# Identity products ahead of transposed scores, two scatters in flight, and a group of heads weighed at once, in a two-layer adaLN kernel

## The chip, the cores and the metric

The kernel runs on one core of a Trainium2 chip. The metric is the time of one execution in microseconds, the lower the better. TensorE multiplies, VectorE and ScalarE work elementwise, GpSimd fills tables and issues the indirect transfers, SyncE issues the plain ones.

## The reference

2,048 tokens of 128 channels go through two layers, each with an attention-like part and a mixture of experts, each part on a layer norm with a modulation (scale, shift, gate).

- Layer 0, attention: the tokens are taken as sequences, and only the first 256 to 309 rows take part. 16 heads of 8 channels. Three passes: a query is projected and normalised for each head, scores against all keys in a window are taken through a softmax, the values are weighed, and the result is added to the query. The window of the next pass is 256, 281 or 309 rows, by how much the result moved.
- Layer 0, experts: softmax router, two of eight experts for each token, 128 to 512 to 128 channels with GELU.
- Layer 1, in place of attention: a linear recurrence with 32 complex modes. Experts: one of eight, ReLU.

```python
scores = einsum('bhqd,bhkd->bhqk', sq, sk) * inv_sqrt_e      # in the window
probs = softmax(scores, axis=-1)
out = einsum('bhqk,bhkd->bhqd', probs, vp)
...                                                            # three passes
y = einsum('nec,ne->nc', out_of_experts, combine)              # two of eight experts
```

## The kernel before

All engines run their own written-out program; semaphores order them. 16 tiles of 128 tokens. The first three tiles (`NA = 3`, "near") take part in attention; the other 13 ("far") do not, and are made ready while attention runs.

**The three passes** (`attend(it)` on each engine). In a pass `nj` is the number of query or key tiles (2, 3, 3) and `nw` the window (256, 281, 309). VectorE makes the normalised queries (`head_norm`, `split`) into a stack, which TensorE turns (`turn`), and ScalarE or VectorE copies. Then come the *scores*: for each head TensorE forms `nj` products into PSUM banks `3b .. 3b+2`, `b = h % 2` (`scores`, L1035), and VectorE reduces them to the row maxima (`maxima`, L1775), which are put into the stack and turned in again. Then the *transposed scores* (`scores_t`, L1055): the same products with keys on the partitions, of which ScalarE takes the exponential (L777) as soon as one of the two bank groups is written. TensorE weighs the values with them (`weigh_one`, L1060): each head writes 9 rows at partition `32 q` of a bank, so that four heads share a bank. `weigh_four(g, jk)` does one key tile of the four heads of group `g`. ScalarE copies the bank (`take`, L784), and TensorE turns it out (`turn_out`, L1082) with a map. VectorE then divides and goes on to the next pass.

`fill(bank, count)` (L1015) is a product of the identity with a repeated identity, 512 columns, into a bank that is about to be overwritten; its result is not used. Before the change it stands ahead of the scores of heads 2 to 15 of passes 1 and 2, and in runs at the start of passes.

For the first three groups, `weigh_four` is mixed with the transposed scores of later heads. The last group is done head by head: after head 2 of the group the groups 0 and 1 are turned out, then head 3 is weighed.

**The far rows.** During pass 0 VectorE adds the bias to all of x and normalises the far rows; TensorE and ScalarE run the router between pass 0 and 1; in pass 1 VectorE chooses experts, counts (TensorE, `count("far")`) and computes the row that each token has in the sorted buffer (`place`). Then GpSimd writes the far rows there with an indirect transfer of 128 rows for each tile and choice, 2 x 13 = 26 (`send_row`, L585). Each waits until the one before has landed. After the first 13 a column of the rows is rewritten (`set_places`). SyncE waits for all 26 (`wait_scattered`) and then loads sorted tiles of 128 rows.

**The experts** (`experts(l)`): turn a tile (L1231), four products up (L1247), bias on VectorE (L1920), activation on ScalarE, four products down (L1258). They start after the attention output was added to the near rows and these are normalised, all on VectorE ahead of its first expert bias. The near rows are routed during the first nine tiles. Layer 1 then follows with a scatter of its own, 16 transfers with no wait between them.

## Time and profile before

| | us |
|---|---|
| three timed runs | 446.42, 459.40, 461.73 |
| their median | 459.4 |
| the profiled execution | 444.71 |
| its span, first to last instruction | 442.7 |
| TensorE, VectorE busy in it | 309.9, 304.5 |
| mean granted TensorE clock in it | 0.822 of 2.4 GHz |

The profile is of one execution. Busy times overlap between engines and do not add up to the span.

### The profile page before, as it was taken

The page shows a single profiled execution, that of the slowest core. Times are in us where ns is not written, and L with a number is a line of the kernel's source. Part 1 is how long each engine was busy: PE and PEld are TensorE (multiplying, and loading weights), DVE is VectorE, ACT ScalarE, POOL GpSimd, SP SyncE. Part 2 cuts the span into 40 slices and gives each one's busy share as a digit, 9 for nine tenths or more (in the row PEclk, how much of TensorE's full clock was granted, in tenths as well). Part 3 has the DMA queues.
Part 4 walks back from the last instruction along what each step waited for, and adds up shares of the span by engine and source line. Part 5 has one row for each costly group of instructions (what it writes and reads, how often), then busy time and mean ns, then how long its engine had stood idle before and what let it go on. Part 6 is the DMA issues. An engine that isn't in the chain of part 4 may idle for free.

```text
span 442.7 us, 7609 instructions
## 1 busy us (share of the span) xinstructions
PE 309.9 (70%) x2168; PEld 222.3 (50%) x2169; DVE 304.5 (69%) x859; ACT 172.0 (39%) x331; POOL 172.4 (39%) x281
## 2 busy tenths in 40 slices
PE   1896888788997889778788999216807200699960
PEld 1672216332353322478788999203807100689960
DVE  7598985995869994268755666566979760277850
ACT  1134553217601268053354555846024600345520
POOL 9572880740133344303575455300000087044560
PEclk9997559697999988969899999758775555699995
DMA  2599800000000000031224220694000022323310
GB/s 79 94 365 371 243 3 1 0 1 1 8 24 24 32 18 26 29 59 44 60 62 79 70 68 28 180 305 135 0 1 1 0 75 106 89 67 82 96 51 0
DMA packets 37805, 32.93 MB, mean 74 GB/s; under 512 B 10765, under 2 KB 28770, under 8 KB 37776
## 3 DMA queue, kind: packets, MB, share of 16 engines
q1 hardware_dynamic: 33792, 25.10, 20.3%
q0 software_dynamic: 3936, 7.49, 5.4%
q8 instruction: 13, 0.21, 0.2%
q14 instruction: 16, 0.13, 0.1%
q10 hardware_dynamic: 48, 0.00, 0.0%
HBM read 19.50 MB, written 13.98 MB: 76 GB/s over the span
## 4 chain that ended last, share of the span: by engine, by line
PE 36%; DVE 24%; DMA 18%; issue 7%; ACT 6%; POOL 4%; SPq 2%; DVEq 1%; POOLq 0%
DMA rows<-token_rows,posu 15%; PE ps L1247 12%; PE ps L1258 10%; POOL rows L585 4%; DVE mx L1775 3%; PE ps L1060 3%; PE ps L1055 2%; PE ps L1035 2%; DVE stats L1383 2%; PE ps L1231 2%; DMA xs<-rows 2%; SPq L293 1%; DVE wide L2017 1%; PE ps L1215 1%; DVE hb L1920 1%
## 5 line engine op out<-in xcount | busy, mean ns | idle before, releaser
L585 POOL DMA_INDIRECT rows<-token_rows,posu x48 | 50.5, 1053 | 142.3 <-DVE token_rows L1698 71.4
L1258 PE MATMUL ps<-w_out,hg 128*128 x496 | 66.1, 278 | 0.0
L1920 DVE TENSOR_TENSOR hb<-ps,b_in 128x512 f32<-128x512 f32 x62 | 42.7, 688 | 31.7 <-PE ps L1247 31.3
L1258 PEld LDWEIGHTS ps<-w_out,hg 128*128 128x128 f32 x496 | 61.0, 194 | 0.2
L597 POOL DMA_INDIRECT back<-ys,places x39 | 38.5, 988 | 48.5 <-DVE ys L1931 43.4
L866 ACT ACTIVATE hg<-hb 128x512 f32<-128x512 f32 x62 | 39.1, 630 | 37.5 <-DVE hb L1920 32.9
L1775 DVE TENSOR_REDUCE mx<-ps 128x2 f32<-128x512 f32 (+2 forms) x48 | 44.1, 947 | 2.3 <-PE ps L1035 1.7
L1247 PE MATMUL ps<-xsT,w_now 128*128 128x128 f32 x256 | 39.2, 302 | 5.9 <-DVE hb L1920 3.7
L1231 PE MATMUL ps<-ident,xs 128*128 128x128 f32 x62 | 18.1, 296 | 35.1 <-DMA xs<-rows 35.1
L1247 PEld LDWEIGHTS ps<-xsT,w_now 128*128 128x128 f32 x256 | 35.2, 213 | 7.5 <-issue 5.1
L765 ACT COPY qs<-ps 128x768 bf16<-128x768 bf16 (+1 forms) x21 | 15.3, 729 | 59.7 <-PE ps L1004 59.7
L597 POOL DMA_INDIRECT out<-ys,rest x23 | 22.6, 984 | 33.2 <-DVE ys L1939 29.3
L1247 PE MATMUL ps<-xsT,qs 128*128 128x128 f32 x240 | 32.1, 277 | 1.0 <-DVE hb L1920 1.0
L1015 PE MATMUL ps<-identb 128*128 128x512 bf16 x98 | 27.5, 392 | 5.6 <-DVE mx L1775 5.2
L1055 PE MATMUL ps<-qs,feat 64*128 64x281 bf16 (+2 forms) x128 | 26.8, 348 | 5.3 <-ACT wide L777 4.1
L1247 PEld LDWEIGHTS ps<-xsT,qs 128*128 128x128 f32 x240 | 29.5, 194 | 1.1 <-issue 1.1
L857 ACT ACTIVATE xsT<-ps,modcol 128x128 f32<-128x128 f32 x39 | 17.7, 454 | 30.3 <-PE ps L1231 30.2
L1931 DVE TENSOR_TENSOR ys<-ps,b_out 128x128 f32<-128x128 f32 x62 | 17.9, 289 | 16.1 <-PE ps L1258 15.0
L777 ACT ACTIVATE wide<-ps 128x512 f32<-128x512 f32 (+2 forms) x36 | 27.5, 819 | 3.6 <-PE ps L1055 3.6
L1231 PEld LDWEIGHTS ps<-ident,xs 128*128 128x128 f32 x62 | 9.4, 152 | 36.2 <-issue 34.2
L1060 PE MATMUL ps<-wide,vpx 128*9 128x281 f32 (+2 forms) x192 | 27.1, 526 | 0.1
L1035 PE MATMUL ps<-feat,qs 64*128 64x281 bf16 (+2 forms) x128 | 24.7, 319 | 3.3 <-DVE mx L1775 1.9
(390 smaller groups left out, 570.4 us busy)
## 6 DMA issues: line engine op xcount, KB each, us to landing
rows<-blank SPq DMA_DIRECT2D x20, 260.0 KB, 7.3
xs<-rows SPq DMA_DIRECT2D x62, 64.0 KB
w_in<-in_L_ffn_w_fc SPq DMA_DIRECT2D x1, 2048.0 KB, 15.1
w_in<-in_L_ffn_W SPq DMA_DIRECT2D x1, 2048.0 KB, 10.5
rest<-rows SPq DMA_DIRECT2D x23, 65.0 KB
token_rows<-in_L_attn_x SPq DMA_DIRECT2D x1, 832.0 KB, 8.1
wmod<-in_L_wmod SPq DMA_DIRECT2D x2, 384.0 KB, 4.3
rows<-token_rows,posu POOLq DMA_INDIRECT x48, 2.4
```

Of the source, the lines that this page charges most:

```text
L585: pool.indirect_dma_start(ROWS[l], bass.IndirectOffsetOnAxis(ap=posu[:, k, j:j + 1], axis=0), token_rows[:, j, 0:WIDTH[l]], None).then_inc ...
L597: pool.indirect_dma_start(where, bass.IndirectOffsetOnAxis(ap=target[r] if l else places[:, t, :].bitcast(U32)[:, 0:1], axis=0), ys[:, r, ...
L777: act.activation(probs[h % NPROBS][:, 0:nj, 0:nw], ps[:, 3 * b:3 * b + nj, 0:nw], ACT.Exp).then_inc(sem("probs_ready"), 1)
L866: act.activation(hg[:, c % RING, :], hb[:, c % 2, :], fn).then_inc(sem("hg_ready"), 1)
L1035: mm = pe.matmul(ps[:, 3 * b + j, 0:nw], half(qs, h)[:, j * P:(j + 1) * P], half(ks, h)[:, 0:nw], start=True, stop=True)
L1055: mm = pe.matmul(ps[:, 3 * b + j, 0:nw], half(ks, h)[:, j * P:(j + 1) * P], half(qs, h)[:, 0:nw], start=True, stop=True)
L1060: return pe.matmul(ps[OROW * q:OROW * q + HD + 1, 6 + g % 2, 0:nw], vpx[:, jk, h, :], probs[h % NPROBS][:, jk, 0:nw], start=(jk == 0), sto ...
L1231: pe.transpose(ps[:, 4 + c % 2, 0:P], xs[:, c % RING, :], ident[:]).then_inc(sem("xs_used"), 1)
L1247: mm = pe.matmul(ps[:, b, n * P:(n + 1) * P], w_ring[c % RING][:, n * P:(n + 1) * P], xsT[:, c % 2, :], start=True, stop=True)
L1258: mm = pe.matmul(ps[:, 6 + c % 2, 0:D], hg[:, c % RING, n * P:(n + 1) * P], w_out[:, bass.ds(e * NB + n, 1), :], start=(n == 0), stop=(n = ...
L1775: v.tensor_reduce(mx[:, 0:nj, h:h + 1], ps[:, 3 * b:3 * b + nj, 0:nw], AX.X, ALU.max).then_inc(sem("max_free"), 1)
L1920: v.tensor_tensor(hb[:, c % 2, :].rearrange("p (b t) -> p b t", b=NB), ps[:, c % RING if h_bank(l, t) is None else h_bank(l, t), :].rearra ...
```

## The change

1. `scores` puts an identity product ahead of heads 2 to 15 in pass 0 too (14 more). `scores_t` puts one ahead of heads 0 to 7, in all three passes (24 more).
2. The far transfers alternate between two semaphores. Each waits only for the one before the last, so two are in flight. Between the two halves both semaphores are waited for, as before; SyncE waits for both.
3. The last group of heads is weighed as the others are, with three (or two) calls of `weigh_four`, after groups 0 and 1 are turned out. `turn_out(0)` now waits for the exponential of head 14, the last even one, and `weigh_four(3, 0)` for that of head 15.

```diff
@@ wait_scattered (SyncE)
-                    sp.wait_ge(sem("scattered_" + g), 16 * (hi - lo) * experts)
+                    n = (hi - lo) * experts
+                    if g == "far":
+                        sp.wait_ge(sem("scattered_odd"), 16 * (n // 2))
+                        n -= n // 2
+                    sp.wait_ge(sem("scattered_" + g), 16 * n)
@@ send_row (GpSimd)
-                                        token_rows[:, j, 0:WIDTH[l]], None).then_inc(sem("scattered_" + g), 16)
+                                        token_rows[:, j, 0:WIDTH[l]], None).then_inc(sem("scattered_odd" if odd else "scattered_" + g), 16)
@@ the far scatter (GpSimd)
-                    pool.wait_ge(sem("scattered_far"), 16 * sent)
+                    pool.wait_ge(sem("scattered_far"), 16 * (sent - sent // 2))
+                    pool.wait_ge(sem("scattered_odd"), 16 * (sent // 2))
                     set_places(NA, NT, N)
                     pool.wait_ge(sem("places_set"), 3)
                 for j in range(NA, NT):
-                    if j > NA:
-                        pool.wait_ge(sem("scattered_far"), 16 * sent)
-                    send_row("far", 0, k, j)
+                    if sent > 1:
+                        pool.wait_ge(sem(("scattered_far", "scattered_odd")[sent % 2]), 16 * (sent // 2))
+                    send_row("far", 0, k, j, odd=bool(sent % 2))
                     sent += 1
@@ scores (TensorE)
-                        if it and h >= 2:
+                        if h >= 2:
                             fill(3 * b, 1)
@@ scores_t (TensorE)
+                        if h < 8:
+                            fill(3 * b, 1)
@@ the end of attend (TensorE)
-                pe.wait_ge(sem("o_taken"), G0 + 2)
-                for q in range(4):
-                    if q == 3:
-
-                        turn_out(0)
-                        turn_out(1)
-                    pe.wait_ge(sem("probs_ready"), H0 + 13 + q)
-                    for jk in range(nj):
-                        mm = weigh_one(3, q, jk)
-                mm.then_inc(sem("weighed"), 1)
+                pe.wait_ge(sem("probs_ready"), H0 + HEADS - 1)
+                turn_out(0)
+                turn_out(1)
+                for jk in range(nj):
+                    weigh_four(3, jk)
                 turn_out(2)
                 turn_out(3).then_inc(sem("o_turned"), 1)
```

## Rows read from the trace of the kernel before

**Rows 1.** The chain that ended last, in time: start us, us, what

```profile
118.44 3.14 DMA rows<-token_rows,posu
...
186.52 2.29 DMA rows<-token_rows,posu
188.82 1.80 DMA xs<-rows
```

**Rows 2.** Timeline of VectorE: start us, us, instruction, [idle before, releaser]

```profile
188.15 0.56 DVE L1880 TENSOR_TENSOR token_rows<-token_rows,ps 128x384 f32<-128x384 f32 x1 [1.74 <-PE ps L1208]
...
191.58 0.86 DVE L1402 TENSOR_SCALAR token_rows<-token_rows,mv,rstd 128x128 f32<-128x128 f32 x3
...
193.97 0.69 DVE L1920 TENSOR_TENSOR hb<-ps,b_in 128x512 f32<-128x512 f32 x1 [0.61 <-PE ps L1247]
```

**Rows 3.** Windows: us, busy time of PE, PEld, DVE, ACT, POOL, granted clock, DMA

```profile
42.00:66.00 24.00, 20.57 (x117) 5.20 (x116) 22.00 (x75) 13.92 (x25) 19.05 (x53) 0.50 0.49 150
80.00:84.00 4.00, 3.77 (x21) 1.79 (x19) 3.61 (x11) 0.80 (x1) 3.82 (x5) 0.50 0.00 0
84.00:100.00 16.00, 13.22 (x84) 5.46 (x80) 15.67 (x20) 3.19 (x4) 9.79 (x8) 0.99 0.00 1
104.00:112.00 8.00, 7.33 (x48) 1.91 (x52) 2.22 (x12) 5.13 (x8) 0.00 (x0) 0.57 0.01 2
162.00:169.00 7.00, 7.00 (x47) 1.46 (x46) 6.79 (x9) 4.38 (x6) 3.62 (x3) 0.55 0.07 21
```

**Rows 4.** The chain that ended last, in the scatter of layer 1

```profile
363.69 0.96 POOL rows L585
364.95 0.96 POOL rows L585
```

**Rows 5.** Timelines of TensorE and ScalarE, end of pass 2

```profile
175.05 2.00 PE L1060 MATMUL ps<-wide,vpx 128*9 128x309 f32 x16
...
178.29 1.55 PE L1082 MATMUL ps<-omap,wmod 128*128 128x68 f32 x12
179.77 1.73 PE L1060 MATMUL ps<-hg,vpx 128*9 128x309 f32 x6
181.43 1.55 PE L1082 MATMUL ps<-omap,wmod 128*128 128x68 f32 x12
...
175.21 0.94 ACT L777 ACTIVATE hg<-ps 128x927 f32<-128x927 f32 x1 [0.18 <-PE ps L1055]
```

**Rows 6.** Timeline of TensorE, pass 1

```profile
81.53 1.91 PE L1015 MATMUL ps<-identb 128*128 128x512 bf16 x4
...
108.03 1.13 PE L1060 MATMUL ps<-wide,vpx 128*9 128x281 f32 x8
109.09 0.88 PE L1055 MATMUL ps<-qs,feat 64*128 64x281 bf16 x3
...
117.04 0.66 PE L1060 MATMUL ps<-wide,vpx 128*9 128x281 f32 x8
117.63 0.53 PE L1055 MATMUL ps<-qs,feat 64*128 64x281 bf16 x3
118.09 0.66 PE L1060 MATMUL ps<-wide,vpx 128*9 128x281 f32 x8
...
124.06 1.55 PE L1082 MATMUL ps<-omap,wmod 128*128 128x68 f32 x12
```

**Rows 7.** Timelines of VectorE and TensorE, pass 0

```profile
42.61 2.07 DVE L1775 TENSOR_REDUCE mx<-ps 128x2 f32<-128x512 f32 x3
...
45.75 2.08 DVE L1775 TENSOR_REDUCE mx<-ps 128x2 f32<-128x512 f32 x3
...
70.90 0.19 DVE L1715 TENSOR_SCALAR den<-ps 128x32 f32<-128x32 f32 x1 [5.42 <-PE ps L1082]
...
62.64 0.60 PE L1055 MATMUL ps<-qs,feat 64*128 64x256 bf16 x2 [0.74 <-ACT wide L777]
...
64.14 0.60 PE L1055 MATMUL ps<-qs,feat 64*128 64x256 bf16 x2
```

More of the change, by code:

```diff
@@ L581, in ready_to_send, with send_row @@
                 pool.wait_ge(sem(f"cleared{l}"), 16 * clears(l))
-            def send_row(g, l, k, j):
+            def send_row(g, l, k, j, odd=False):
                 pool.indirect_dma_start(ROWS[l], bass.IndirectOffsetOnAxis(ap=posu[:, k, j:j + 1], axis=0),
-                                        token_rows[:, j, 0:WIDTH[l]], None).then_inc(sem("scattered_" + g), 16)
+                                        token_rows[:, j, 0:WIDTH[l]], None).then_inc(sem("scattered_odd" if odd else "scattered_" + g), 16)
             def send_tile(l, t):
```

## The prediction

> **What bounds the kernel now.** I read the chain of work that ended last first. From 118 to 189 us it is one thing, the scatter of the far token rows: 26 transfers from 118.44 to 186.52 us, a mean spacing of 68.08 / 25 = 2.72 us, each step being a landing of about 2.29 us and then the next issue, and behind the last one the first load of sorted rows at 188.82 us [rows 1]. The reader is to see that nothing of TensorE or VectorE stands in the chain there. Second, the timelines of VectorE and TensorE at the same place, to see what is late next: the third attention pass ends with the add of 188.15 us and a layer norm until 191.58 + 0.86 = 192.44 us, and the first expert bias comes at 193.97 after only 0.61 us of waiting for TensorE [rows 2]. So scatter and attention tie: making the scatter alone shorter frees about 3 us, making the attention alone shorter frees nothing once the scatter is issued. What is worth something is both together. Third, the windows with the granted clock: TensorE stands at half speed (1.2 GHz) from 42 to 66 us, at 80 to 84, and for most of 104 to 112 and 162 to 169 us [rows 3].
>
> **Two far transfers in flight.** Removed: 24 of the 26 waits for the transfer before; added: a wait for the last but one. A transfer lands 2.29 us after its issue and the wait and issue around it take 0.26 more. With two in flight the spacing is the larger of 2.55 / 2 = 1.28 us and what GpSimd itself needs. The second layer's scatter shows the latter without any wait between issues: 363.69 to 364.95 us, 1.26 us, with rows twice as wide [rows 4]. I take 1.3 us, bounds 1.26 (GpSimd) and 2.55 (no overlap), nearer the lower one because the only row without waits shows it. The drain between the two halves stays, so 26 x 1.3 + 3 = 37 us instead of 70.4. Behind these waits GpSimd has the sends of the first expert results, due only once the experts run, and SyncE the row loads, which want the scatter done anyway, so nothing else is delayed. The saving, 33 us, is not the gain: the attention pass covers all but the last 3 us. It only takes the scatter out of the way of what follows.
>
> **The last four heads weighed together.** In pass 2 the last weighing of the third group starts at 175.05 and takes about 0.7 us; from there the serial form (three heads, the turning out of two groups, the fourth head) lasts until 181.43: 5.7 us. The new order is the turning out of groups 0 and 1, 179.77 - 178.29 = 1.48 us, and three four-head weighings of 0.66 us (0.73 at 309 columns) [rows 5, 6], 3.4 to 3.7 us. Saved: 2.0 to 2.3, I take 2.2. Pass 1 by the same rows: from 118.09 + 0.66 to 124.06 is 5.3 us, the new order 1.48 + 3 x 0.6 = 3.3; saved 2.0. The added wait, all four exponentials before any of the weighing, costs nothing as long as the turning out covers it: the last exponential ends at 175.21 + 0.94 = 176.15 us [rows 5], the turning out would run to about 177.2; if that cover were gone, it would cost at most the 0.9 us of one exponential. Behind it on TensorE only the end of the pass is queued. Pass 0 has two key tiles instead of three; its small saving (0 to 1 us) falls under the cap below. What is late next is ScalarE's copy of the last group, which keeps its place, and then VectorE, which idles in front of it in every pass.
>
> **Identity products, passes 1 and 2.** Eight more of 512 columns in each pass, ahead of heads 0 to 7 of the transposed scores. At half speed four take 1.91 us, 0.48 each [rows 6]; at full speed I halve that, 0.24. What they may buy is the half-speed stretch that follows. A pair of weighing and scores costs 1.13 + 0.88 us at half speed and 0.66 + 0.53 at full [rows 6], 0.47 and 0.35 less. The stretch of pass 1 holds three weighings and four scores: 3 x 0.47 + 4 x 0.35 = 2.8 us, minus the four products that now stand in it, 4 x 0.24: 1.9 us. Pass 2 has a stretch of about the same length; I allow 0.2 us for products that ScalarE has to wait for ahead of it: 1.7 us. Bounds for each pass: +3.4 (the whole stretch at double speed, products hidden) and -3.8 (8 x 0.48, no change of clock and no cover). Why near the upper end: from 84 to 100 us the products of the first scores hold 0.99 with TensorE 83% busy, and this cadence is what the transposed scores now get; in the 4 us before, dense products at half speed were followed by full speed [rows 3].
>
> **Identity products, pass 0.** 14 in front of the scores and 8 in front of the transposed scores. The pass enters the scores at half speed. There VectorE's reductions set the pace, four heads in 45.75 - 42.61 = 3.14 us [rows 7]; with a product per head TensorE needs about 0.48 for the two score products of 256 columns (together one identity product long), 0.48 for the identity product and 0.1 for its share of the turning, 1.05 us per head, so it becomes the bound and each head loses 0.25 us until the clock rises. I put the rise 4 to 7 us later, as at 80 to 84 us [rows 3]: 1.0 to 1.7 us lost, and about 0.07 per head won afterwards because the waits of VectorE go: net -0.9 us. The transposed part now takes 1.50 us per head from head 6 on (62.64 to 64.14) [rows 7], all of it TensorE at half speed; at 2.4 GHz it takes half, 0.75, or up to 0.85 where ScalarE sets the pace (my allowance), over ten heads 6.5 to 7.5 us less. Not all counts. VectorE does the layer norm of the far rows meanwhile and is idle only 5.42 us before it takes the result at 70.90 [rows 7]; that idle time is a cap on everything saved in the second half of pass 0, the new weighing included. So pass 0 gives 5.4 - 0.9 = 4.5 us; bounds -5 (no rise) and +5.4.
>
> Of this part the Trainium skill says in "TensorE: Matmul & The Clock Gate", Terms, that the penalty of the throttle is about the time throttled times what is missing of the clock. By it pass 0 alone would give 24 x 0.5 = 12 us; the 5.42 us of VectorE speak against that in this kernel.
>
> **Entry to the experts.** With the far rows long in memory the first turned tile no longer waits for a load. TensorE would have the first tiles' products ready when the layer norm ends, and VectorE's 0.61 us of waiting goes [rows 2], and some of that before the second and third bias. The sum of the removed waits is at least 0.6 and at most 2.7 (TensorE's turn is set by a load that came 188.82 + 1.80 = 190.62, against an attention end near 188) [rows 1, 2]; I take 1.5. From there on the order of work is unchanged and I carry the gain through to the end.
>
> **The sum.** 4.5 (pass 0) + 1.9 + 2.0 (pass 1) + 1.7 + 2.2 (pass 2) + 1.5 (entry) = 13.8 us. The check on the scatter: it can start 4.5 + 1.9 = 6.4 us earlier, at 112.0, and ends near 149; the attention ends near 188.0 - 12.3 = 175.7. The scatter would bind again only above (175.7 - 112.0) / 26 = 2.45 us per transfer. The profiled execution took 444.7 us with a span of 442.7; it goes to 430.9, span 428.9. The three timed runs are 446.4, 459.4 and 461.7, so the profile belongs with the lowest, and the median is 3% above it; the traces do not say why. From the lowest run the sum gives 432.6, which is my forecast, 433; from the median it would give 445.6, which the range must hold. A gain below about 2%, 9 us, could not be told from none.
>
> **Pass 0 stays at half speed.** For it: that pass ran at 0.50 for 24 us though TensorE was 86% busy [rows 3]. Against: with the products it becomes the bound, and is idle no more. It would lose 14 x 0.25 + 8 x 0.2, about 5 us, instead of winning 4.5: 13.8 - 9.5 = 4.3 saved, 440. Chance 0.15.
> **Slower: the products never lift the clock and nothing hides them.** Place: before the exponentials, where ScalarE waits for each score. Price: 5 us in pass 0 and 3.8 in each of the others, with the half-speed stretches kept, against 4.2 from the weighing and 1.5 at the entry: 12.6 - 5.7 = 7 us slower, 452. It decides from the point at which fewer than about one in two of the 38 products is covered. Chance 0.05.
> **The transfers do not overlap.** The change then does not do what it says: spacing 2.55, the scatter ends 6.4 us earlier and no more, and so does the start of the experts: 438. Against: the scatter of the second layer [rows 4]. Chance 0.08.
> **The clock counts in full.** All half-speed time is halved: 12 + 3.4 + 3.1 us, and 5.7 for weighing and entry: 24 us, 420. This is what the rule cited above amounts to. It would need VectorE's work in pass 0 off the path [rows 7]. Chance 0.05.
> The forecast has 0.60; the rest, 0.07, is anything else.
>
> **How the numbers follow.** Low end 425: the upper bounds of passes 1 and 2 and of the entry. High end 449: the forecast counted from the median of the runs with some of the fills uncovered, the half-speed rival included. Faster by over 2%: the forecast, the full clock and the part of the others that lies beyond, 0.72; within 2%: 0.23; slower 0.05.
>
> **What would show it.** Right: far scatter of about 37 us with spacings of 1.3; granted clock 1.0 from about 46 us on in pass 0 and through the transposed scores of passes 1 and 2; TensorE's last turning out within 4 us of the last group's third weighing; VectorE idle under 1 us before it takes the result of pass 0; the first turned tile right behind the attention output. Wrong: 0.50 anywhere in the transposed scores, or a longer mean of the exponential's waits without a higher clock, or a later wait in the experts that takes back what the entry gained.

## The result, and the profile after

The changed kernel takes 473.12 us (median of four executions, 467.11 to 477.58) against 455.27 us of the kernel before (446.42 to 461.73): a ratio of 1.050 with a 95% interval of 1.027 to 1.072. Every ratio here leaves out executions that lie well above the fastest of their kernel, so it is not the quotient of the two medians, which is 1.039. The kernel is slower, outside my range of 425 to 449. The profiled execution took 477.58 us, the highest of its four, as that of before was the lowest of its own, so the two spans (475.9 and 442.7 us) lie 33 us apart where the medians lie 18: what the two profiles differ by is more than the change costs on the median.

The page of the changed kernel: span, busy time, and the granted clock in tenths in 40 slices.

```profile
span 475.9 us, 7691 instructions
PE 346.6 (73%) x2206; PEld 229.5 (48%) x2207; DVE 304.1 (64%) x859; ACT 173.3 (36%) x331; POOL 170.3 (36%) x281
PEclk9796556755589955597997999975775555599995
```

TensorE is busy 37 us longer with 38 more small products, which alone would be 9 to 21 us (38 at 0.24 to 0.54): the rest is the same work at a lower clock, 0.745 on the mean against 0.822. The windows say where. Columns as in [rows 3]; the first answers to its 42:66, the third and fourth are the scores (all but their first 2.3 us) and transposed scores of pass 1, the last two those of pass 2.

```profile
42.00:66.00 24.00, 24.00 (x93) 6.19 (x91) 18.04 (x57) 9.95 (x16) 18.07 (x53) 0.50 0.51 158
66.00:80.00 14.00, 12.57 (x82) 3.90 (x77) 4.87 (x20) 6.08 (x14) 0.91 (x2) 0.51 0.00 1
97.00:117.00 20.00, 20.00 (x77) 7.09 (x76) 14.20 (x17) 2.42 (x4) 7.26 (x6) 0.50 0.00 0
117.00:132.00 15.00, 15.00 (x68) 4.19 (x69) 4.45 (x20) 8.85 (x11) 0.00 (x0) 0.50 0.01 1
162.00:185.00 23.00, 21.91 (x86) 7.54 (x83) 17.86 (x19) 3.41 (x6) 10.64 (x11) 0.57 0.21 44
185.00:203.00 18.00, 18.00 (x83) 4.66 (x86) 13.25 (x23) 11.12 (x13) 0.00 (x0) 0.51 0.00 1
```

Passes 1 and 2 enter their scores (94.67 and 162.00) at full speed and lose it there, near 97 and 165 us. It comes back in the later part of each pass only, near 134.4 and 202.7 us. Narrow windows around the two falls:

```profile
94.00:96.00 2.00, 0.80 (x9) 0.43 (x7) 1.93 (x4) 0.80 (x1) 1.82 (x3) 1.00 0.00 0
96.00:98.00 2.00, 1.91 (x9) 0.62 (x9) 1.68 (x2) 0.00 (x0) 2.00 (x2) 0.71 0.00 0
164.00:166.00 2.00, 1.86 (x12) 0.92 (x11) 2.00 (x3) 0.15 (x1) 1.36 (x3) 0.78 0.11 33
```

The first window of the table above is the surprise: TensorE is busy for 24.00 of 24 us, where it was 20.57, and the clock stays at 1.2 GHz throughout; VectorE, the bound before with 22.00, is down to 18.04. The timeline of TensorE there:

```profile
42.75 0.61 PE L1040 MATMUL ps<-feat,qs 64*128 64x256 bf16 x2
43.29 0.61 PE L1020 MATMUL ps<-identb 128*128 128x512 bf16 x1
43.83 0.61 PE L1040 MATMUL ps<-feat,qs 64*128 64x256 bf16 x2
44.37 0.61 PE L1020 MATMUL ps<-identb 128*128 128x512 bf16 x1
```

Starts are 0.54 us apart, so a head takes 1.08 us where VectorE could take one in 3.14 / 4 = 0.79 [rows 7]. VectorE's wait for the result of the pass, 5.42 us in [rows 7], is now 10.07:

```profile
81.18 0.19 DVE L1717 TENSOR_SCALAR den<-ps 128x32 f32<-128x32 f32 x1 [10.07 <-PE ps L1089]
```

The scatter does what the change says. Its issues on GpSimd, which answer to [rows 1], are mostly 1.28 us apart (2.56 before; 2.72 on the mean, the drain between the halves included), and it is issued in 36.7 us, from 138.9 to 175.5. The first load of sorted rows starts at 177.9, long before the last add of the attention at 218.6:

```profile
147.06 0.97 POOL L589 DMA_INDIRECT rows<-token_rows,posu  x1 [0.30 <-DMA rows<-token_rows,posu]
148.34 0.97 POOL L589 DMA_INDIRECT rows<-token_rows,posu  x1 [0.31 <-issue]
149.63 0.98 POOL L589 DMA_INDIRECT rows<-token_rows,posu  x1 [0.32 <-issue]
...
175.52 0.97 POOL L589 DMA_INDIRECT rows<-token_rows,posu  x1 [0.31 <-issue]
```

So does the weighing. TensorE at the ends of pass 1 and pass 2, against [rows 6] and [rows 5]: from the last weighing of the third group (139.14 and 208.00) to the last turning out (142.76 and 211.80) it is 3.0 and 3.1 us where it was 5.3 and 5.7. But in pass 1 TensorE stops in the middle of that turning out:

```profile
139.14 0.66 PE L1067 MATMUL ps<-wide,vpx 128*9 128x281 f32 x8
139.73 1.55 PE L1089 MATMUL ps<-omap,wmod 128*128 128x68 f32 x12
...
142.76 0.89 PE L1089 MATMUL ps<-omap,wmod 128*128 128x68 f32 x6
145.79 0.89 PE L1089 MATMUL ps<-omap,wmod 128*128 128x68 f32 x6 [2.15 <-issue]
...
208.00 0.71 PE L1067 MATMUL ps<-wide,vpx 128*9 128x309 f32 x8
208.63 1.55 PE L1089 MATMUL ps<-omap,wmod 128*128 128x68 f32 x12
...
211.80 1.55 PE L1089 MATMUL ps<-omap,wmod 128*128 128x68 f32 x12
```

It waits for ScalarE's copy of the last group. That copy, ready to go when the weighing ended near 142.8, runs only at 145.34, 2.5 us late, and the releaser named is none of this core's engines:

```profile
145.34 0.39 ACT L789 COPY wmod<-ps 128x281 f32<-128x281 f32 x1 [4.88 <-remote]
```

At the entry to the experts VectorE no longer waits for TensorE, as forecast (0.61 us in [rows 2], nothing here):

```profile
218.59 0.56 DVE L1882 TENSOR_TENSOR token_rows<-token_rows,ps 128x384 f32<-128x384 f32 x1 [1.81 <-PE ps L1210]
...
223.72 0.68 DVE L1922 TENSOR_TENSOR hb<-ps,b_in 128x512 f32<-128x512 f32 x1
```

I followed one set of milestones through every profile: the first and last row maximum of a pass, the start of VectorE's `den` that takes the pass's result, the far counts (after the transposed scores of pass 1), the first expert bias. The table gives the time from one to the next, in us, read from the timelines (two ways between passes, 13.5 and 14.6 us before, are left out); "1/2" marks stages at half speed, or at half speed but for their first 2 to 4 us. Each column is one execution: "after" the longest of its four, "no scatter" the shortest of its six. Forecasts are the terms of the prediction.

| stage | before | after | forecast | before again | no scatter edit |
|---|---|---|---|---|---|
| pass 0, scores | 12.1 | 17.9 | | 12.1 | 17.5 |
| pass 0, from last maximum to result | 19.9 | 24.4 | (pass 0: -4.5) | 20.5 | 25.1 |
| pass 1, scores | 16.9 | 22.6 (1/2) | | 16.9 | 16.9 |
| pass 1, transposed scores | 10.1 | 14.6 (1/2) | -1.9 | 10.1 | 8.6 |
| pass 1, weighing to result | 14.3 | 15.8 | -2.0 | 14.6 | 11.8 |
| pass 2, scores | 17.4 | 23.3 (1/2) | | 17.4 | 17.4 |
| pass 2, from last maximum to result | 25.3 | 28.1 | -3.9 | 25.3 | 21.4 |
| result of pass 2 to first bias | 10.9 | 10.3 | -1.5 | 13.1 | 20.2 |
| end of span | 442.7 | 475.9 | | 450.6 | 456.8 |

### The profile page after: what moved, and what is told of

Same layout as the page of the kernel before. It is cut to its first block, busy times and chain, and to the rows that moved or that the text cites. A ratio compares the mean times of both kernels' runs of the same rounds, so it can differ in the third digit from the quotient of the medians.

```text
span 475.9 us, 7691 instructions
## 1 busy us (share of the span) xinstructions
PE 346.6 (73%) x2206; PEld 229.5 (48%) x2207; DVE 304.1 (64%) x859; ACT 173.3 (36%) x331; POOL 170.3 (36%) x281
## 4 chain that ended last, share of the span: by engine, by line
PE 50%; DVE 26%; issue 9%; POOL 5%; ACT 2%; DMA 2%; DVEq 2%; SPq 1%; another core or an unknown queue 1%; POOLq 0%
PE ps L1249 9%; PE ps L1260 7%; PE ps L1020 7%; PE ps L1040 6%; PE ps L1062 6%; PE ps L1067 5%; POOL rows L589 3%; DVE hb L1922 2%; PE ps L1009 2%; PE ps L1089 2%; DVE stats L1385 2%; SPq L293 1%; POOL out L601 1%; DVE wide L2019 1%; PE ps L1217 1%
## 5 line engine op out<-in xcount | busy, mean ns | idle before, releaser
L589 POOL DMA_INDIRECT rows<-token_rows,posu x48 | 49.4, 1030 | 122.4 <-DVE token_rows L1700 71.6
L1922 DVE TENSOR_TENSOR hb<-ps,b_in 128x512 f32<-128x512 f32 x62 | 42.5, 686 | 33.4 <-PE ps L1249 25.1
L1020 PE MATMUL ps<-identb 128*128 128x512 bf16 x136 | 56.3, 494 | 2.7 <-DVE mx L1777 2.5
L1777 DVE TENSOR_REDUCE mx<-ps 128x2 f32<-128x512 f32 (+2 forms) x48 | 45.2, 950 | 18.2 <-PE ps L1040 16.8
L1040 PE MATMUL ps<-feat,qs 64*128 64x281 bf16 (+2 forms) x128 | 34.5, 403 | 1.0 <-DVE qs L1763 1.0
L601 POOL DMA_INDIRECT out<-ys,rest x23 | 22.6, 983 | 33.3 <-DVE ys L1941 22.6
L1062 PE MATMUL ps<-qs,feat 64*128 64x281 bf16 (+2 forms) x128 | 32.1, 395 | 1.4 <-ACT wide L782 0.7
L782 ACT ACTIVATE wide<-ps 128x512 f32<-128x512 f32 (+2 forms) x36 | 28.6, 807 | 12.1 <-PE ps L1062 12.1
L1020 PEld LDWEIGHTS ps<-identb 128*128 128x128 bf16 x136 | 14.5, 108 | 35.4 <-DVE mx L1777 11.7
L1933 DVE TENSOR_TENSOR ys<-ps,b_out 128x128 f32<-128x128 f32 x62 | 17.8, 287 | 18.4 <-PE ps L1260 14.2
L862 ACT ACTIVATE xsT<-ps,modcol 128x128 f32<-128x128 f32 x39 | 17.5, 452 | 32.4 <-PE ps L1233 26.4
## 6 DMA issues: line engine op xcount, KB each, us to landing
w_in<-in_L_ffn_W SPq DMA_DIRECT2D x1, 2048.0 KB, 10.3
```

The lines of the kernel that those rows point to most:

```text
L589: pool.indirect_dma_start(ROWS[l], bass.IndirectOffsetOnAxis(ap=posu[:, k, j:j + 1], axis=0), token_rows[:, j, 0:WIDTH[l]], None).then_inc ...
L601: pool.indirect_dma_start(where, bass.IndirectOffsetOnAxis(ap=target[r] if l else places[:, t, :].bitcast(U32)[:, 0:1], axis=0), ys[:, r, ...
L782: act.activation(probs[h % NPROBS][:, 0:nj, 0:nw], ps[:, 3 * b:3 * b + nj, 0:nw], ACT.Exp).then_inc(sem("probs_ready"), 1)
L1020: pe.matmul(ps[:, bank, :], identb[:], identb[:].unsqueeze(1).to_broadcast([P, 4, P]), start=True, stop=True)
L1040: mm = pe.matmul(ps[:, 3 * b + j, 0:nw], half(qs, h)[:, j * P:(j + 1) * P], half(ks, h)[:, 0:nw], start=True, stop=True)
L1062: mm = pe.matmul(ps[:, 3 * b + j, 0:nw], half(ks, h)[:, j * P:(j + 1) * P], half(qs, h)[:, 0:nw], start=True, stop=True)
```

## The experiments

Every run is told with its median, the number of executions, and the ratio to the kernel before on the same chip. The edits are pieces of the change on the kernel before unless the text says otherwise.

### The kernel before again

> The kernel before once more, for a second profile. If the first profile was a lucky one (theory H: full speed through the scores of passes 1 and 2 is chance), this one has at least one of the two at 0.50 and 22.7 us in place of 16.9 there, and takes 450 to 462 us. If not, it takes about 445 us with the same stretches of half speed.

453.14 us (n 11), ratio 0.997 [0.992, 1.002]. Its profile has a span of 450.6 us with a clock of 0.80. In the runs beside the parts the kernel before had 78 more executions between 446.7 and 466.8 us. The profile from which I forecast, 444.71 us, was below every one of them. Its 8 us are hardly in the passes (0.9 up to the result of pass 2) but from the entry to the experts on. So the starting point of the forecast was about 10 us too low, whatever the change did.

### One part alone: products in pass 0

```diff
-                        if it and h >= 2:
+                        if h >= 2:
                             fill(3 * b, 1)
```

> The kernel before with the 14 identity products ahead of the scores of pass 0 and nothing else. Theory A (at half speed a stream of identity products and score products does not raise the clock): pass 0 stays at 0.50 and each head of the scores takes 1.09 us instead of 0.79, about 4 to 5 us slower. Theory C (the half speed of pass 0 in the changed kernel was chance of that one profile): the clock rises within 7 us and the kernel gains up to 5 us.

456.64 us (n 4), ratio 1.008 [1.001, 1.016]. Scores of pass 0: 17.9 us, as in the changed kernel; the rest of the pass as before (20.0); pass 1 and 2 unchanged (16.9, 17.4). The clock is 0.50 from 42 to 66 us. The step "I put the rise 4 to 7 us later" fails already here, alone.

### One part alone: products ahead of the transposed scores

```diff
                             pe.wait_ge(sem("qs_act"), C0 + 4 + h // 4)
+                        if h < 8:
+                            fill(3 * b, 1)
```

> The kernel before with the 24 identity products ahead of the transposed scores and nothing else. Theory A: pass 0 is at half speed there, 8 products of 0.54 us are paid in full or nearly, 3 to 4 us slower in pass 0; in passes 1 and 2 they hold full speed if the clock is there and cost up to 4 us if it is not; in all 2 to 8 us slower. Theory D (they hold the clock in passes 1 and 2, as was forecast): pass 0 loses 3 us and passes 1 and 2 give 3 to 4 back, no difference.

458.77 us (n 4), ratio 1.012 [1.003, 1.020]. The profile is of the longest of the four. Pass 0, from last maximum to result: 24.5 us for 19.9, so eight products at half speed, 8 x 0.54 = 4.3, and nothing hides them. In pass 1 the clock fell inside the scores, at about 97 us (20.3 us for 16.9), and the transposed scores ran at half speed, 14.6 us for 10.1. Without these products they take 10.5 us at half speed (the profile of the two transfers in flight alone), so at that clock eight products cost 4.0 us there. In pass 2 at full speed they gained 1.4 us, near the forecast 1.7.

### The clock warm when pass 0 begins

Weighing and scatter as changed, products in the scores of pass 0, none ahead of the transposed scores, and a longer run of products at the start of the pass.

```diff
                     pe.wait_ge(sem("ks_act"), 4)
+                    fill(4, 5)
...
-                            fill(4, (12, 0, 44)[it])
+                            fill(4, (22, 0, 44)[it])
```

> The two other edits, the 14 products ahead of the scores of pass 0, and 15 more at the start of pass 0 that fill TensorE's idle time of 2.3 and 1.0 us there, so that the clock need not fall before the scores. Theory A (the products can hold full speed but not restore it): pass 0 at 1.00 through its scores at 0.72 us per head, and some way into the transposed scores; 3 to 8 us faster than the two edits alone in pass 0. Theory C' (products next to half-array score products can do neither): 0.50 from 40 us on, as in the changed kernel, 4 us slower than the two edits alone.

461.79 us (n 4), ratio 1.024 [1.007, 1.041], the denser scatter included. The windows, scores of pass 0 first, then the transposed part:

```profile
40.00:52.00 12.00, 10.99 (x64) 3.93 (x63) 10.81 (x19) 5.56 (x9) 5.69 (x24) 1.00 1.05 333
55.00:72.00 17.00, 15.57 (x102) 5.64 (x101) 11.13 (x49) 7.71 (x16) 11.19 (x24) 0.51 0.00 1
```

Entered at full speed, the mix held 1.00 here through the scores of pass 0; entered at half speed it held 0.50. And full speed buys nothing: the scores take 12.0 us for 12.1, since VectorE sets their pace (10.81 of 12 us busy). The clock fell again 3 us after them, at 55 us, when the weighing had started. That full speed is held is no rule: in pass 1 of this same profile the clock fell inside the scores, near 93 us.

### Four products a head in pass 0

```diff
-                        if it and h >= 2:
-                            fill(3 * b, 1)
+                        if h >= 2:
+                            fill(3 * b, 1 if it else 4)
```

> The kernel before with four identity products ahead of each of heads 2 to 15 of the scores of pass 0. Theory A1 (they can raise the clock if they are dense enough): 1.00 within some 7 us of their start, pass 0 then paced by 4 x 0.21 + 0.3 us per head, 1 to 5 us slower in all. Theory A2 (they cannot, whatever their number): 0.50 through all of them, 2.2 us per head and 20 us slower.

467.81 us (n 2), ratio 1.028 [1.017, 1.040]. TensorE at the point where the clock rises:

```profile
42.02 1.89 PE L1015 MATMUL ps<-identb 128*128 128x512 bf16 x4
43.84 0.61 PE L1035 MATMUL ps<-feat,qs 64*128 64x256 bf16 x2
44.38 0.61 PE L1004 MATMUL ps<-identb,stack 128*128 128x128 bf16 x4
44.78 1.34 PE L1015 MATMUL ps<-identb 128*128 128x512 bf16 x4
46.06 0.39 PE L1035 MATMUL ps<-feat,qs 64*128 64x256 bf16 x2
46.38 1.04 PE L1015 MATMUL ps<-identb 128*128 128x512 bf16 x4
```

Here it does rise, near 45 us; so the clock can be lifted in this stage, only not by one product a head. The price is a head every 1.29 us, 22.9 us for the scores, and at 66 us the clock is at half again.

### Products of ones in place of the identity

The changed kernel, with other data in the unused products only.

```diff
-                    pe.matmul(ps[:, bank, :], identb[:], identb[:].unsqueeze(1).to_broadcast([P, 4, P]), start=True, stop=True)
+                    pe.matmul(ps[:, bank, :], onesb[:], onesb[:].unsqueeze(1).to_broadcast([P, 4, P]), start=True, stop=True)
```

> The changed kernel with all its extra products taken as ones times ones instead of identity times identity; same sizes, same places. Theory F (what counts as activity is the data, and an identity is nearly all zeros): the clock rises in the scores of pass 0 and stays up, 10 to 25 us faster than the changed kernel. Theory G (the data do not matter): same time and same half-speed stretches as the changed kernel, about 473 us.

470.92 us (n 4), ratio 1.037 [1.014, 1.060]. The same window, the same picture, busy all the time at 0.50:

```profile
42.00:66.00 24.00, 24.00 (x91) 6.42 (x93) 17.76 (x55) 9.48 (x16) 17.60 (x52) 0.50 0.49 153
```

So the zeros of the identity are not what keeps the clock down in the scores of pass 0. Behind them this profile differs: the clock rises near 67 us, in the transposed scores (0.99 from 67 to 75), which none of the three profiles with identity products in both places shows before 78. Whether that is the data or chance, one profile does not tell.

### No products between heads

The kernel before without those it has in the scores of passes 1 and 2.

```diff
-                        if it and h >= 2:
-                            fill(3 * b, 1)
```

> The kernel before without the identity products that stand ahead of single heads in the scores of passes 1 and 2 (the runs of them at the start of passes stay). Theory A (bistable: with a product per head TensorE paces the scores at 1.36 us per head when at half speed and 1.05 when at full, without one VectorE paces them at 1.05 in either): scores of passes 1 and 2 at 1.05 us per head whatever the clock, spread of the runs smaller, median 0 to 6 us below the kernel before. Theory E (those products keep the clock up and are worth it): more half speed in the later part of each pass, 3 to 8 us slower.

456.91 us (n 4), ratio 1.012 [0.998, 1.027]. The scores of pass 1, at half speed for most of their time (0.58 on the mean), take 17.5 us: VectorE's pace, 0.6 us from full speed. Those of pass 2 take 18.4 for 17.4. With products they take 16.9 at full speed and 22.6 at half (table). So a product a head has two outcomes in these passes and is no insurance: in pass 1 it wins 0.6 us where the clock holds and costs 5.1 where it doesn't. The half-speed outcome is the one that lasts: once the clock had fallen inside these scores, no profile with products shows it back before they ended, and it fell there in the changed kernel and in several of its parts.

### One part alone: two transfers in flight

```diff
-                    if j > NA:
-                        pool.wait_ge(sem("scattered_far"), 16 * sent)
-                    send_row("far", 0, k, j)
+                    if sent > 1:
+                        pool.wait_ge(sem(("scattered_far", "scattered_odd")[sent % 2]), 16 * (sent // 2))
+                    send_row("far", 0, k, j, odd=bool(sent % 2))
```

> The kernel before with the two far transfers in flight and nothing else. Theory A (the identity products are what costs): the scatter shrinks from 70 to about 37 us, the attention pass covers all but the last 3 us of it, 0 to 3 us faster than before, and no new stall. Theory B (the denser scatter delays other transfers, the instruction fetch among them, as in the stall of 2 us while it ran in the changed kernel): 3 to 8 us slower, with idle time in the trace that no semaphore explains.

462.39 us (n 4), ratio 1.010 [0.996, 1.023]: no gain, though the scatter is issued in 37.3 us for 68.1. The profile is of the longest of the four. It names "issue" as the releaser of waits of, among others, 1.1 us on TensorE, 4.5 on VectorE and 4.7 on ScalarE in the stretch of the scatter, where the profiles of before and of the eight runs that keep its scatter have at most 0.2 us of that kind. Most of it is no delay. ScalarE's copy of the last group, in before and here:

```profile
124.16 0.39 ACT L784 COPY wmod<-ps 128x281 f32<-128x281 f32 x1 [4.74 <-PE ps L1060]
...
134.36 0.39 ACT L789 COPY wmod<-ps 128x281 f32<-128x281 f32 x1 [4.74 <-issue]
```

The same wait of 4.74 us, at the same place, ends at TensorE's product in one and has no name in the other. The same holds for the 1.1 us on TensorE (1.13 before, for VectorE), and VectorE's 4.5 us end 0.1 us after TensorE's turning out, as before. So a wait is to be compared with the same wait of before, not counted by its name. What is later in the way from pass 1 to pass 2 is 0.9 us in all, 15.5 us for 14.6.

Pass 2 then goes through its scores at half speed, 23.3 us for 17.4 (pass 1 did too, 22.7, ahead of the scatter):

```profile
155.00:175.00 20.00, 20.00 (x73) 6.66 (x71) 14.76 (x18) 3.17 (x5) 7.74 (x8) 0.50 0.22 45
```

### No wait at all between the transfers of a half

```diff
-                    if j > NA:
-                        pool.wait_ge(sem("scattered_far"), 16 * sent)
```

> The kernel before with no wait between the 13 transfers of a half (up to 13 in flight). Theory B (the fewer gaps the indirect transfers leave, the longer the instruction fetches of the other engines wait): more unexplained idle time on ScalarE, VectorE and TensorE from the start of the scatter on than with two in flight, and slower than before by 2 to 8 us. If GpSimd's own 1.27 us per transfer is what spaces them, the same as with two in flight. If theory B is wrong: no such idle time.

468.59 us (n 5), ratio 1.036 [1.026, 1.046], with one semaphore and no other edit. Up to the scatter (118.5 us) every milestone is that of before. Then VectorE's reductions of pass 2 stop, with no instruction of the profile to wait for:

```profile
147.41 1.13 DVE L1773 TENSOR_REDUCE mx<-ps 128x3 f32<-128x927 f32 x1 [0.30 <-PE ps L1033]
153.78 1.12 DVE L1773 TENSOR_REDUCE mx<-ps 128x3 f32<-128x927 f32 x1 [5.24 <-issue]
154.82 0.19 DVE L1767 CAST stack<-mx 128x12 bf16<-128x12 f32 x1
155.89 2.15 DVE L1773 TENSOR_REDUCE mx<-ps 128x3 f32<-128x927 f32 x2 [0.89 <-remote]
```

The scores of pass 2 take 28.7 us for 17.4, and the way into them 17.9 for 14.6. VectorE could start at 149.5, when the products were written, so it is 4.3 us late, and TensorE stands behind it:

```profile
154.96 0.61 PE L1013 MATMUL ps<-identb 128*128 128x512 bf16 x1 [5.48 <-DVE mx L1773]
```

The clock was 1.00 until this stop, falls near 152.5 us in it, and stays at 0.50 to the end of the scores. One wait was taken away, on GpSimd alone, so the denser transfers stop engines that have no part in them; this run alone does not tell their spacing from their number in flight.

### Two in flight, but spaced out

A memset of 0.54 us on GpSimd ahead of each transfer, into a buffer that is not in use yet.

```diff
+                    if j > NA:
+                        then(pool.memset(xs[:], 0.0))
                     send_row("far", 0, k, j, odd=bool(sent % 2))
```

> The kernel before with two far transfers in flight, but GpSimd clears an unused tile of 512 columns (about 0.7 us with its wait) between two issues, spacing some 2 us instead of 1.28. Theory B1 (the spacing is what counts): no unexplained waits on ScalarE and VectorE in pass 2, the scatter ends some 12 us earlier, pass 2 at full clock, the start of the experts 2 to 3 us earlier: 0 to 3 us faster than before. Theory B2 (two in flight is what counts): waits as with the unpaced scatter, 3 to 10 us slower.

454.33 us (n 11), ratio 1.009 [1.002, 1.015]. The spacing is 1.79 us (rows of it below, under the best version), the scatter is still issued in 49 us, and the scores of pass 2 keep their pace, 17.4 us at 1.00. The way from pass 1 to pass 2 is 15.9 us for 14.6. That is the price of the memset: VectorE's own instructions are slower while GpSimd writes. Four of them that compute `feat` take 2.51 us here for 1.88 in the repeated profile of before, and under the weighing as well three copies into the stack take 1.34 for 0.60. In this profile the spacing matters more than that two are in flight; the next paced kernels show how far that carries. It wins nothing alone, since the attention is next.

### The weighing alone

```diff
-                pe.wait_ge(sem("o_taken"), G0 + 2)
-                for q in range(4):
-                    if q == 3:
-
-                        turn_out(0)
-                        turn_out(1)
-                    pe.wait_ge(sem("probs_ready"), H0 + 13 + q)
-                    for jk in range(nj):
-                        mm = weigh_one(3, q, jk)
-                mm.then_inc(sem("weighed"), 1)
+                pe.wait_ge(sem("probs_ready"), H0 + HEADS - 1)
+                turn_out(0)
+                turn_out(1)
+                for jk in range(nj):
+                    weigh_four(3, jk)
```

> The kernel before with the last four heads weighed together and nothing else. Theory A as forecast: about 2 us less in each of passes 1 and 2 and no unexplained wait of ScalarE at the end of pass 1, but the scatter then binds the start of the experts: 0 to 4 us faster. Theory B' (that wait of 2 us at the end of pass 1 comes from the shorter weighing that no longer hides a fetch of instructions, not from the scatter): it is in this trace too.

455.59 us (n 11), ratio 1.004 [0.998, 1.010]. Pass 1, weighing to result: 12.0 for 14.3; pass 2, from last maximum to result: 23.3 for 25.3. So 2.3 and 2.0 us, where 2.0 and 2.2 were forecast. ScalarE's copy of the last group in pass 1 starts 0.13 us after TensorE goes on to the turning out, where it is 2.58 us in the changed kernel, so that delay does not come from the shorter weighing. Nothing reaches the end: the scatter, issued until 190.6, sets the start of the experts, as [rows 1] and [rows 2] said it would.

### Weighing and scatter, without the new products

The two edits above together.

> The changed kernel without its 38 new identity products; those of passes 1 and 2 that were there before stay. Theory A: it loses nothing and gains what the other two edits are worth, 4 to 9 us faster than before. Theory B: the scatter costs, so it is no faster than before.

457.44 us (n 4), ratio 1.008 [0.998, 1.018]. Both sides of the tie are shorter, and it is no gain. In the profile, the longest of the four, ScalarE's first copy of pass 2 starts 1.6 us after the turning that it waits for (at once in before), TensorE then stops for 2.08 us in the scores of pass 2, and the clock falls in that stop. Pass 1 is at half speed throughout. The scores take 23.1 and 24.1 us.

The same, with the edit under "No products between heads" too:

> Both other edits of the change (two far transfers in flight, last four heads weighed together) and no identity product ahead of single heads anywhere. Theory A: as the kernel without these products, and 4 to 8 us less for the two edits, some 445 us with little spread. Theory E: the half speed costs what the two edits gain, no better than before.

459.24 us (n 4), ratio 1.018 [1.003, 1.032]. Pass 1 at half speed is now 17.6 us, but pass 2, in the scatter, 23.7, where the kernel without products and with the old scatter takes 18.4: even without products the stalls stretch it.

### Weighing without products between heads

The edit of the weighing and the one of "No products between heads", with the old scatter.

> The last four heads weighed together, the scatter one by one as before, and no identity product ahead of single heads. Theory A and B together: 2 us less in each pass, scores at VectorE's pace in any clock, no unexplained waits; the scatter hides what pass 2 saves. 0 to 5 us faster than before. Theory E (the products earn their time by the clock): slower than before by 2 to 5 us.

452.97 us (n 11, 450.46 to 455.27), ratio 1.002 [0.997, 1.006]. No faster than before, but its eleven executions spread by 4.8 us only, against 11 to 20 of the kernel before in the five groups of runs: what sets the two outcomes apart is gone. The scores of pass 1 take 17.8 us, at half speed but with VectorE busy for 15.38 of 17 us:

```profile
86.00:103.00 17.00, 14.02 (x69) 6.07 (x68) 15.38 (x19) 3.20 (x4) 9.09 (x7) 0.50 0.00 0
```

### Spaced scatter and weighing, with and without products between heads

The edits named, each as shown above.

> The same paced scatter, with the last four heads weighed together. Theory B1: the 2 us that the weighing saves in each of passes 1 and 2 and the 2 to 3 us at the start of the experts now all reach the end, 4 to 7 us faster than before. Theory B2: slower by 2 to 8 us.

With the products of before: 455.50 us (n 11), ratio 0.996 [0.989, 1.002]. Its profile shows where the spacing does not help: the scores of passes 1 and 2 take 23.2 and 24.3 us. The way into pass 2 is 16.9 us for 14.3 with the weighing alone, by VectorE's slower instructions; TensorE stands idle for 2.29 us behind them (1.06 in before), and the clock falls from 1.00 to 0.50 there, at 143 us.

> The same, and no identity product ahead of single heads in any pass. Theory A: scores at VectorE's pace whatever the clock, so a smaller spread and a median 0 to 4 us under that of the kernel that keeps them. If the clock matters more in the later parts: 0 to 4 us over it.

Without them: 449.46 us (n 5, 447.33 to 452.46), ratio 0.989 [0.981, 0.998]. This has the lowest median of all versions, 7 us under the kernel before beside it; by the ratio it is 1%, about 5 us, with five executions and an interval that only just leaves out no gain. GpSimd in its scatter:

```profile
139.35 0.97 POOL L589 DMA_INDIRECT rows<-token_rows,posu  x1 [0.28 <-POOL xs L688]
140.32 0.54 POOL L688 MEMSET xs<- 128x512 f32 x1
141.14 0.97 POOL L589 DMA_INDIRECT rows<-token_rows,posu  x1 [0.28 <-POOL xs L688]
```

Its mean clock, 0.763, is lower than that of the kernel before (0.80 in the repeated profile) and it is faster: the reader is to see that the mean clock is no measure by itself. The way into pass 2 is long here too, 16.7 us, and TensorE idles as it does with the products; without them the half speed that follows costs 1.1 us (18.5 for 17.4). The first bias comes at 194.1 us, for 197.1 in the repeated profile of before.

### The change without one of its parts

Products and weighing, with the scatter of the kernel before.

> The changed kernel with the old far scatter, one transfer at a time: all 38 new products and the new weighing. Theory 1, the dense scatter disturbs the other engines: without it passes 1 and 2 are as with the transposed products alone (pass 2 scores 17.4 us at full speed, no waits named issue on TensorE in the scatter), ratio to the kernel before about 1.015 to 1.02, and the change with it costs about 3 per cent more. Theory 2, the products are the whole loss: ratio 1.04 to 1.05, pass 2 scores at half speed and near 23 us.

462.79 us (n 6), ratio 1.020 [1.011, 1.030]. The last column of the table is its profile. Its windows, pass 0, then scores and transposed scores of pass 1, then from the scores of pass 2 on:

```profile
42.00:66.00 24.00, 24.00 (x91) 5.97 (x88) 18.07 (x58) 10.06 (x16) 18.32 (x53) 0.50 0.50 156
...
95.00:112.00 17.00, 14.21 (x92) 6.05 (x90) 16.70 (x20) 3.69 (x5) 9.59 (x8) 1.00 0.00 0
112.00:121.00 9.00, 8.46 (x67) 3.25 (x66) 4.42 (x21) 7.82 (x11) 0.00 (x0) 1.00 0.01 2
147.00:164.00 17.00, 14.34 (x88) 5.75 (x85) 16.91 (x19) 3.73 (x6) 6.95 (x8) 1.00 0.07 24
164.00:186.00 22.00, 20.93 (x180) 8.49 (x178) 13.59 (x25) 16.52 (x22) 9.28 (x7) 1.00 0.07 23
```

Here the mechanism that I forecast for passes 1 and 2 is at work: 10.1 - 8.6 = 1.5, 14.3 - 11.8 = 2.5 and 25.3 - 21.4 = 3.9 us, together 7.9 where the prediction has 1.9 + 2.0 + 3.9 = 7.8. It only cannot pay: pass 0 is 10.6 us longer, so the scatter starts at 127.7 instead of 118.4, one at a time ends after 198.4, and the experts wait for it. This is the shortest of its executions; two of the six took 472 and 474 us.

The whole change, with the memset ahead of each transfer:

> The changed kernel with a memset ahead of each far transfer, so that they come about 1.8 us apart, still two in flight. Theory 1, it is the close spacing that costs: the waits shrink, pass 2 scores stay near 17.4 us, ratio 1.015 to 1.025. Theory 2, two in flight as such or the products cost: ratio 1.04 to 1.05 as in the change itself.

462.43 us (n 12), the kernel before beside it 459.10 (n 16); the changed kernel with the old scatter, above, had 462.79. There is no ratio on record, and the executions lie far apart: 446.57 to 478.24, the widest spread of any kernel here. They order roughly by clock: 0.832 in the lowest, 0.752 and 0.753 in the two highest. One program, outcomes 30 us apart. In its profile pass 1 is at half speed and pass 2 at full (22.1 and 17.4 us for the scores), and from the last maximum of pass 2 to the result it takes 21.4 us, as without the scatter edit. The spread leaves the share of the spacing in the full change unsettled.

## Why the prediction was wrong, point by point

**The starting point.** Counted from the profile, 444.71, or the lowest timed run. The kernel before has its median near 455, so 433 should have been about 441 with the same sum. The rivals' times (440, 452, 438, 420) were counted from 444.7 and the forecast from 446.4, so they are not on one scale. I had written down the 3% between profile and median and placed the forecast at the wrong end of it.

**The step that failed: "I put the rise 4 to 7 us later".** In pass 0 it never comes. I took 80 to 84 us of [rows 3] as the example, but those four products are a run of identity products by themselves; in pass 0 each is followed by as long a stretch of score products on 64 of the 128 rows. The rival "pass 0 stays at half speed" (chance 0.15) had the mechanism and a price too low. It has 14 x 0.25 + 8 x 0.2, about 5 us. Measured: a head is 0.54 + 0.54 and a share of 0.11 in the turning, 1.19 us against 0.79, 14 x 0.40 = 5.6 in the scores (17.9 - 12.1 = 5.8), and 8 x 0.54 = 4.3 ahead of the transposed scores (24.4 - 19.9 = 4.5). The whole pass costs 10.3 us instead of giving 4.5. It is 10.3 to 10.8 us in the three profiles with both sorts of identity product, and 5.6 with ones, where the clock was back at full from 67 us on.

**The argument against that rival, "with the products it becomes the bound, and is idle no more".** It did become the bound, 24.00 of 24 us, and the clock did not move. The Trainium skill has in "TensorE: Matmul & The Clock Gate", Part 1, that activity releases the throttle. By the busy share of the profile this case does not agree in pass 0: 24.00 of 24 us busy, at 0.50. The denser products of one experiment did release it.

**Passes 1 and 2.** The gain is real where the clock holds, 7.9 us for 7.8. That "the products of the first scores hold 0.99" [rows 3] was right as a reading and wrong as a guarantee: in the profile of the changed kernel the clock fell near the start of both scores, which then took 5.7 and 5.9 us more, and the transposed scores of pass 1 took 4.5 more. For pass 1 the cause is open. It begins before the scatter, and the profiles with the scores of pass 1 at 22 us and more include kernels without any new product.

**Pass 2 goes with the scatter.** The profiles of kernels that have products between heads sort themselves. With the far transfers one at a time the scores of pass 2 take 17.3 to 17.4 us in all seven, the one with a slow pass 1 included. With the denser transfers they take 23.3 to 28.7 us in all six, the one with a pass 1 at full speed included. All six are at 1.00 at the start of these scores, and the clock falls 3 to 13 us in. In three of them it falls in a stop of TensorE, of 2.08, 3.40 and 5.48 us; in the other three, the changed kernel among them, no stop stands there. So by these thirteen profiles about 6 us of pass 2 belong to the denser scatter. Spaced out, two profiles of three keep 17.4.

**The scatter.** Spacing 1.3 forecast, 1.28 measured; 37 us forecast in place of 70.4 up to the first load of sorted rows, 39.0 measured. Waits at the entry as forecast: 0.6 us to the first bias and 1.6 more until the near rows are counted, 2.2 for 1.5. The sentence "nothing else is delayed" failed: it looked at what is queued behind the waits on GpSimd and SyncE and not at what the denser transfers do to engines that have no part in them. In the changed kernel this is 2.15 us in pass 1, the 5.9 us of pass 2 above and, by the drop of the ratio from 1.050 to 1.020 without the scatter edit, up to 3% in all; the two intervals just overlap.

**The weighing.** Forecast 2.0 and 2.2, measured 2.3 and 2.0 alone.

**The sum.** In the profiles the first bias comes 223.7 - 194.0 = 29.7 us later: pass 0 10.3, pass 1 10.2 and 1.5, pass 2 8.7, the ways between and the entry -0.9. The remaining 3.5 us lie behind it, where the repeated profile of the kernel before is as long. This is the account of the longest execution. Of the 18 us between the medians, pass 0 is the 10 that all three profiles with identity products in both places show. The point from which the slower rival decides was named, "fewer than about one in two of the 38 products is covered". It happened: none of the 22 in pass 0 was covered, and its chance, 0.05, should have been several times that.

**Open:** what the engines wait for during closely spaced transfers (the profile says "issue" and "remote"; late instructions, which three expectations name, were not tested), what decides between the two outcomes of pass 1, and how the denser transfers lower the clock in pass 2 where TensorE does not stop. Nor is it shown why the clock stays down in pass 0 while TensorE is busy all the time: the score products there use 64 of the 128 rows, and no run puts others in their place.

## What to carry to other kernels

A filler product on an engine that is throttled is paid at the throttled price, so first ask what it costs if the clock does not move, and put that number in the sum; add it only where another engine's pace covers it even then. Where a stage has two outcomes, taking out what makes the slow one expensive (here the products between heads) narrowed the spread to 5 us at no cost that the runs show, and nothing here that tried to secure the fast one gained; a gain of about 1% came only with the spaced scatter and the weighing as well. And when a queue of transfers is shortened that was not alone on the path, shorten it only as far as is needed: 1.8 us apart served the same end as 1.28. And a wait without a name in a profile is first to be laid beside the same wait of the kernel before: here most of them were as long there.

## What was not expected of the hardware

- TensorE fully busy in the records for 24 us and more with 512-column bf16 products alternating with products on 64 rows stays at 1.2 GHz (0.50); the same mix entered at 2.4 GHz stayed there for the 12 us of pass 0 in one profile, and fell within 3 to 13 us in pass 2 of six. With four such products to one pair it rose, near 45 us, while the third group of four ran.
- Changing between the two kinds costs: 0.54 us from start to start for one 512-column product at half speed, against (43.84 - 42.02) / 4 = 0.46 in a run of four.
- Indirect transfers of 128 rows 1.3 us apart bring stops of up to 5.24 us on VectorE and starts up to 2.5 us late on ScalarE, though neither touches them, and TensorE's clock falls in the scores beside them in six profiles of six, against none of seven with the transfers one at a time. At 1.79 us apart these scores take their old 17.4 us in two profiles of three.
- A memset of 0.54 us on GpSimd every 1.8 us makes short instructions of VectorE longer: three copies of 128x384 bf16 take 1.34 us for 0.60.
- One program spreads by up to 32 us from execution to execution on the same chip, and the order roughly follows its mean granted clock.
